# A fused kernel's head: other idle products on TensorE, expert folds moved among them, three small reorderings

## The chip, the cores and the metric

One NeuronCore of one Trainium2 chip runs the whole kernel in one launch. The metric is the device time of that core in microseconds. Three runs of the kernel before gave 267.57, 268.63 and 270.42 us; the median is 268.63 us.

## The reference, cut to what matters

The kernel computes, in float32, a small conditioning network followed by a feed-forward block on 64 samples of 32 rows with 512 features:

```
h    = gelu(gelu(cond @ W0 + b0) @ W1 + b1)              # 64 x 128
att  = softmax(h @ W2 + b2)                               # 64 x 8
agg_w = einsum('bk,koi->boi', att, weight)                # a 32x32 matrix per sample
agg_b = att @ bias_k                                      # 64 x 32
mix  = einsum('boi,bih->boh', agg_w, x) + agg_b[:, :, None]   # 64 x 32 x 512
shared = relu(mix @ up_w)**2 @ down_w                     # 512 -> 1024 -> 512
routed = ((mix @ fc1_w) @ expert_w * top2_sum(mix @ gate_w)) @ fc2_w
out  = x + layernorm(shared + routed) * gamma + beta
```

## The kernel before, in words

The 2048 rows (64 x 32) are 16 tiles of 128 rows, four tiles to a block, so four blocks of 512 rows. The features lie in four chunks of 128 partitions. The instruction order of each engine is written out by hand and the engines meet at semaphores; each engine runs its own list in order.

**Precision.** A float32 value is split into two fp32r parts, `x_hi` (a cast) and `x_lo` (the difference), and `three_products` (L773 to L776) issues hi*hi, hi*lo and lo*hi, each 128x128 weights by up to 512 columns. Small products (the conditioning network, the mix, the expert fold) run on plain float32 operands; such a product is two records in the trace (x2), since TensorE takes it in two parts.

**The head** is all that comes before the first up product. TensorE: H1 (L725), gelu on ScalarE (L402), H2 (L728), gelu (L404), LOGIT (L732, and its bias b2 as a product with a row of ones, L733), softmax on VectorE and ScalarE (L512, L410, L514, L516), transpose of the attention (L740), split of it on VectorE (L520, L522), the eight aggregation products AGG (L746), which give every sample's 32x32 matrix, the rows of the bias (L752), and AGG_B (L755), the bias broadcast over the first block's columns, whose operand VectorE prepares (L527, L533, L535). ScalarE (L433) and VectorE (L569) copy the aggregated matrices into the block-diagonal tile `mix`. Then `mix_chunk` (L758) multiplies x by it, four tiles for each of four feature chunks, on float32. VectorE adds the bias (`mix_bias`, L556), ScalarE casts (`mix_high`, L425), VectorE subtracts (`mix_low`, L561), and the first block's up products (`up_first_block`, L783) begin. The up weights are split on the way: ScalarE casts a quarter (256 columns, `up_hi`, L416), VectorE subtracts it (`up_lo`, L542), in pieces of 128 columns of which each up group m needs its own.

**Idle products.** `stay_warm(n)` (L711) issues n products on TensorE whose result nobody reads. In the kernel before their weights are `gate_hl[:, 0, :]`, 96 columns of zeros on 128 partitions, and they move 192 columns of the same tile. They stand in the head wherever TensorE waits for another engine or a load.

**The expert fold.** `fold_expert(lc, half, m)` (L716) multiplies expert_w and fc2_w once (eight products of 128x128 weights by 256 columns, float32), into PSUM banks 6 and 7. Its result is first needed in the down stage of block 0. Before, two of the eight stand in the head, one behind the third mix chunk, and five in front of the second half of block 0's up products.

From there on TensorE runs up, latent, gate, mix of the next block, and down, four times; the last normalisation and store close the kernel.

Of the kernel before, what the change touches and what calls it, by code (L numbers as in the profile page):

```python
# [5 lines left out]
def adaln_ffn_kernel(  # L6
# [42 lines left out]
    P = 128  # L49
# [30 lines left out]
    with ctx:  # L80
# [85 lines left out]
        ones = sq_lo[0:2 * K, 1, 0:P]  # L166
        half = sb("half", [P, 1])
        warm = sb("warm", [P, 1])

        ps = ctx.enter_context(nc.psum_tensor("ps", [P, 8, TOK], fp32))  # L170
        H1 = ps[:, 4, 64:64 + NB]
        H2 = ps[:, 4, 128:128 + NB]
        LOGIT = ps[0:NB, 4, 192:192 + K]
        ATT_T = ps[0:SR, 4, 256:256 + NB]
        IDLE = ps[0:GC, 0, 0:2 * GC]
        AGG_B = ps[:, 1, :]
        AGGB_ROWS = ps[0:NB, 3, 0:C]

# [216 lines left out]
        @block.scalar  # L395
        def _(act):

            act.wait_ge(dve_const, 1)
            nc.scalar.activation(warm[:, :], warm[:, :], ACT.Gelu).then_inc(warmed, 1)
            act.wait_ge(mlp_loaded, 16)  # L400
            act.wait_ge(h1_done, 1)
            nc.scalar.activation(hid1[:, :], H1, ACT.Gelu, bias=b0_sb).then_inc(gelu_done, 1)  # L402
            act.wait_ge(h2_done, 1)
            nc.scalar.activation(hid2[:, :], H2, ACT.Gelu, bias=b1_sb).then_inc(gelu_done, 1)  # L404

            act.wait_ge(warmed, 1)
            nc.scalar.activation(warm[:, :], warm[:, :], ACT.Exp).then_inc(warmed, 1)
            act.wait_ge(logit_done, 1)
            act.wait_ge(max_done, 1)
            nc.scalar.activation(att_exp[:, :], LOGIT, ACT.Exp, bias=neg_max[:, :],  # L410
                                 accum_out=exp_sum[:, :]).then_inc(exp_done, 1)

            def split_up(i):
                cols = slice(i * UPC, (i + 1) * UPC)
                act.wait_ge(up_loaded[i], 16)
                nc.scalar.copy(up_hi[:, :, cols], up_raw[:, :, cols]).then_inc(up_hi_ready, 1)  # L416

            def q_high(lc):
                act.wait_ge(q_done, lc + 1)
                nc.scalar.copy(q_hi[:, lc, :], Q[lc]).then_inc(q_hi_ready, 1)  # L420

            def mix_high(b, chunks=range(HC)):
                for c in chunks:
                    act.wait_ge(h_ready, HC * b + c + 1)
                    nc.scalar.copy(h_hi[:, c, :], h_full[:, c % 2, :]).then_inc(h_hi_ready, 1)  # L425

            act.wait_ge(const_ready, 2)
            act.wait_ge(agg_done, 1)  # L430
            for q in (0, 1):
                for g in range(G):
                    nc.scalar.copy(mix_part(g, q), agg_src(q, g, TB)).then_inc(mix0_act, 1)  # L433
            split_up(0)
            act.wait_ge(aggb_done, 1)
            nc.scalar.copy(agg_b[:, 0:TOK], AGG_B).then_inc(aggb_copied, 1)
            act.wait_ge(rows_done, 1)
            nc.scalar.copy(aggb_rows[:, :], AGGB_ROWS).then_inc(rows_copied, 1)
            split_up(1)
            mix_high(0, [0])  # L440
            mix_high(0, [1, 2, 3])
            split_up(2)
            split_up(3)
            for q in (0, 1):
                for g in range(G):
                    nc.scalar.copy(agg_part(g, q), agg_src(q, g, NT)).then_inc(agg_act, 1)
            act.wait_ge(latents_loaded, 16)
            nc.scalar.copy(fc1_hi[:, :, :], fc1_raw).then_inc(fc1_hi_ready, 1)
            act.wait_ge(dve_const, 2)
            nc.scalar.copy(gate_hl[:, :, 0:NE], gate_raw).then_inc(gate_hi_ready, 1)  # L450

            def relu_square(b, m):
                act.wait_ge(up_done, IC * b + m + 1)

                wait_past(act, sq_lo_ready, IC * b + max(m - 1, 0))
                nc.scalar.activation(relu_sq[:, m % 2, :], ps[:, UP_BANK[m], :], ACT.Relu).then_inc(relu_done, 1)  # L456
                act.wait_ge(relu_done, IC * b + m + 1)
                nc.scalar.activation(relu_sq[:, m % 2, :], relu_sq[:, m % 2, :], ACT.Square).then_inc(square_done, 1)  # L458

            def latent_gate(b):  # L460
                for lc in range(LC):
                    act.wait_ge(lat_done, LC * b + lc + 1)
                    nc.scalar.copy(lat_hi[:, lc, :], ps[:, LAT_BANK[lc], :]).then_inc(lat_hi_ready, 1)
                act.wait_ge(gate_done, b + 1)
                nc.scalar.copy(gate_sb, ps[0:2 * NE, GATE_BANK, :]).then_inc(gate_copied, 1)

            def scale_routed(b):
                act.wait_ge(top2_done, b + 1)
                for t in range(TB):
                    act.wait_ge(routed_done, TB * b + t + 1)  # L470

                    wait_past(act, final_done, TB * b + max(t - 1, 0))
                    nc.scalar.mul(y_buf[:, t % 2, :], routed(t), top2[:, t:t + 1]).then_inc(scaled_done, 1)  # L473

            def down_high(i):
                ks = slice(i * DNC, (i + 1) * DNC)
                act.wait_ge(down_loaded[i], 16)
                nc.scalar.copy(down_hi[:, ks, :], down_raw[:, ks, :]).then_inc(down_hi_ready, 1)

            for m in range(IC):  # L480
                relu_square(0, m)
                if m in (0, 1):
                    q_high(m)
                if m in (2, 3, 4, 5):
                    down_high(m - 2)
            latent_gate(0)
            mix_high(1)
            scale_routed(0)
            with act.Fori(1, NBLK - 1) as b:
                for m in range(IC):  # L490
                    relu_square(b, m)
                latent_gate(b)
                mix_high(b + 1)
                scale_routed(b)
            for m in range(IC):
                relu_square(NBLK - 1, m)
            latent_gate(NBLK - 1)
            scale_routed(NBLK - 1)

        @block.vector  # L500
        def _(dve):
            nc.vector.memset(warm[:, :], 0.0).then_inc(dve_const, 1)
            nc.vector.memset(gate_hl[:, :, :].bitcast(mybir.dt.uint32), 0).then_inc(dve_const, 1)
            nc.vector.memset(ones[:, :].bitcast(mybir.dt.uint32), ONE_BITS).then_inc(dve_const, 1)
# [62 lines left out]
            for q in (2, 3):  # L567
                for g in range(G):
                    nc.vector.tensor_copy(mix_part(g, q), agg_src(q, g, TB)).then_inc(mix0_dve, 1)  # L569
            split_up(0, 2)  # L570
            dve.wait_ge(aggb_copied, 1)
            mix_bias(0, 0)
            split_up(2)
            mix_low(0, 0)
            mix_bias(0, 1)
            split_up(3)
            mix_low(0, 1)
# [132 lines left out]
        def _(pe):  # L710
            def stay_warm(n):  # L711

                for i in range(n):
                    nc.tensor.matmul(IDLE, gate_hl[:, 0, :], gate_hl[:, 1:3, :], start=True, stop=True)  # L714

            def fold_expert(lc, half, m):  # L716

# [1 line left out]
                return nc.tensor.matmul(Q[lc][:, cols], expert_T[:, m, lc * P:(lc + 1) * P],  # L719
                                        fc2_raw[:, m, cols], start=(m == 0), stop=(m == LC - 1))  # L720

            pe.wait_ge(dve_const, 3)
            stay_warm(11)
            pe.wait_ge(mlp_loaded, 16)
            nc.tensor.matmul(H1, w0_sb, cond_T, start=True, stop=True).then_inc(h1_done, 1)  # L725
            stay_warm(5)
            pe.wait_ge(gelu_done, 1)
            nc.tensor.matmul(H2, w1_sb, hid1[:, :], start=True, stop=True).then_inc(h2_done, 1)  # L728
            stay_warm(4)
            pe.wait_ge(kernels_loaded, 16)  # L730
            pe.wait_ge(gelu_done, 2)
            nc.tensor.matmul(LOGIT, hid2[:, :], w2_sb, start=True, stop=False)  # L732
            nc.tensor.matmul(LOGIT, ones[0:1, 0:NB].bitcast(fp32), b2_sb, start=False, stop=True).then_inc(logit_done, 1)  # L733
            stay_warm(1)
            pe.wait_ge(experts_loaded, 16)
            fold_expert(0, 0, 0)
            stay_warm(1)
            pe.wait_ge(const_ready, 1)
            pe.wait_ge(att_done, 1)
            nc.tensor.transpose(ATT_T, att[:, :], ident[0:NB, 0:NB]).then_inc(attT_done, 1)  # L740
            fold_expert(0, 0, 1)

            pe.wait_ge(weight_lo_ready, 1)
            pe.wait_ge(att_lo_ready, 1)
            for c in range(C // G):
# [4 lines left out]

            pe.wait_ge(attT_copied, 1)
            nc.tensor.matmul(AGGB_ROWS, att_T[0:K, :], bias_raw[0:K, :], start=True, stop=True).then_inc(rows_done, 1)  # L752
            stay_warm(1)
            pe.wait_ge(attb_lo_ready, 1)
            nc.tensor.matmul(AGG_B, ones[:, :], bias_parts, start=True, stop=True).then_inc(aggb_done, 1)  # L755
            stay_warm(3)

            def mix_chunk(b, c, bank):  # L758
                for t in range(TB):
# [8 lines left out]
            mix_chunk(0, 1, MIX0_BANK[1])  # L768
            pe.wait_ge(h_ready, 1)
            mix_chunk(0, 2, MIX0_BANK[2])  # L770
            fold_expert(0, 1, 0)

            def three_products(dst, a_hi, a_lo, b_hi, b_lo, first, last):  # L773
                nc.tensor.matmul(dst, a_hi, b_hi, start=first, stop=False)  # L774
# [8 lines left out]
            def up_first_block():  # L783

                for c in range(HC):
# [10 lines left out]
                    if c == 0:  # L796
                        pe.wait_ge(h_ready, 2)
                        mix_chunk(0, 3, MIX0_BANK[3])
                fold_expert(0, 1, 1).then_inc(q_done, 1)
                pe.wait_ge(h_ready, 3)  # L800
                for half in (0, 1):
                    for m in range(LC):
# [166 lines left out]
```

## Time and profile before

| | us |
|---|---|
| median of three runs | 268.63 |
| lowest, highest | 267.57, 270.42 |
| span of the profiled execution | 266.2 |
| TensorE busy in it | 259.0 (97%) |
| VectorE, ScalarE, GpSimd busy | 154.9, 85.2, 44.6 |
| first TensorE instruction | 1.49 |
| first mix product, first up product | 13.60, 18.24 |

The profile page has no time of its own for the profiled execution beside its span, from the first to the last instruction, 266.2 us. The three timed runs are 1.37, 2.43 and 4.22 us above it; what lies around the span and what differs from run to run can't be told apart there.

A row of the timeline is: start, duration in us, engine, line, operation, written tile and read tiles, shape. xN means N instructions in a row on that engine with nothing of another kind between them, and the duration is then that of the whole group, from the first start to the last end. Matmuls are pipelined, so the end of one lies after the start of the next; the distance of starts is what a product costs. PEld is the load of a product's weights, a separate instruction that TensorE runs beside the matmuls.

### The profile page before, as it was taken

To read this page: it belongs to the slowest core of one execution; us is meant where nothing else is said; L and a number is where in the kernel's file an instruction comes from. 1 tells how busy PE (TensorE), PEld (TensorE's weight loads), DVE (VectorE), ACT (ScalarE), POOL (GpSimd) and SP (SyncE) were. 2 spreads that over 40 slices of the span, in tenths; PEclk is the share of its full clock that TensorE was granted. 3 is DMA by queue.
4 is the path that set the end of the run, shared out by engine and by line. 5 is a ranking of instruction groups with operands and counts; after the bars stand their busy time and mean duration, and the time that the engine had idled before them with its cause. 6 is when DMAs were issued, how large, how long until landed. Compare 5 with 4: busy or idle time off the path is not lost.

```text
span 266.2 us, 3377 instructions
## 1 busy us (share of the span) xinstructions
PE 259.0 (97%) x1222; PEld 215.7 (81%) x1222; DVE 154.9 (58%) x268; ACT 85.2 (32%) x146; POOL 44.6 (17%) x42
## 2 busy tenths in 40 slices
PE   7999999999999999999999999999999999999991
PEld 7698888788888888888888888888888888778891
DVE  3686899974444954384544963384444963314454
ACT  4356994441111354241110354231110355211110
POOL 1000409101111800001111810001111700001111
PEclk9999999999999999999999999999999999999997
DMA  6973710400111240000111140000111100001111
GB/s 211 342 224 147 264 52 10 151 0 0 42 39 39 49 151 0 0 0 4 39 39 39 42 155 0 0 0 0 39 39 39 42 0 0 0 2 39 39 39 39
DMA packets 9132, 15.71 MB, mean 59 GB/s; under 512 B 634, under 2 KB 3578, under 8 KB 9122
## 3 DMA queue, kind: packets, MB, share of 16 engines
q1 hardware_dynamic: 9122, 15.57, 17.4%
q8 instruction: 7, 0.11, 0.2%
q14 instruction: 3, 0.02, 0.0%
HBM read 11.37 MB, written 4.20 MB: 58 GB/s over the span
## 4 chain that ended last, share of the span: by engine, by line
PE 95%; issue 2%; DVE 1%; POOLq 0%; POOL 0%; DVEq 0%
PE ps L774 26%; PE ps L776 26%; PE ps L775 26%; PE ps L760 6%; PE ps L714 2%; PE ps L719 2%; PE ps L838 1%; PE ps L840 1%; PE ps L746 1%; PE ps L850 1%; POOLq L80 0%; POOL rstd L378 0%; PE ps L755 0%; DVE stats L617 0%; DVE y_buf L615 0%
## 5 line engine op out<-in xcount | busy, mean ns | idle before, releaser
L774 PE MATMUL ps<-down_hi,sq_hi 128*128 128x512 f32 (+1 forms) x136 | 51.3, 377 | 0.0
L775 PE MATMUL ps<-down_lo,sq_hi 128*128 128x512 f32 (+1 forms) x136 | 51.2, 377 | 0.0
L776 PE MATMUL ps<-down_hi,sq_lo 128*128 128x512 f32 (+1 forms) x136 | 51.2, 377 | 0.0
L774 PE MATMUL ps<-h_hi,up_hi 128*128 128x512 f32 x128 | 50.3, 393 | 0.0
L776 PE MATMUL ps<-h_hi,up_lo 128*128 128x512 f32 x128 | 49.8, 389 | 0.0
L775 PE MATMUL ps<-h_lo,up_hi 128*128 128x512 f32 x128 | 49.8, 389 | 0.0
L378 POOL TENSOR_TENSOR rstd<-mv,half 128x1 f32<-128x1 f32 x16 | 15.7, 982 | 177.4 <-DVE mv L622 171.9
L456 ACT ACTIVATE relu_sq<-ps 128x512 f32<-128x512 f32 x32 | 19.1, 597 | 58.1 <-PE ps L776 44.2
L615 DVE TENSOR_TENSOR y_buf<-ps,y_buf 128x512 f32<-128x512 f32 x15 | 10.4, 691 | 45.9 <-PE ps L776 45.9
L589 DVE CAST sq_hi<-relu_sq 128x512 fp32r<-128x512 f32 x32 | 23.6, 737 | 20.9 <-ACT relu_sq L458 20.2
L473 ACT ACTIVATE y_buf<-ps,top 128x512 f32<-128x512 f32 x16 | 11.0, 689 | 69.2 <-PE ps L776 67.2
L591 DVE TENSOR_TENSOR sq_lo<-relu_sq,sq_hi 128x512 fp32r<-128x512 f32 x32 | 31.0, 967 | 1.1
L775 PEld LDWEIGHTS ps<-down_lo,sq_hi 128*128 128x128 f32 x136 | 25.6, 188 | 4.7
L774 PEld LDWEIGHTS ps<-down_hi,sq_hi 128*128 128x128 f32 x136 | 25.6, 188 | 4.7
L776 PEld LDWEIGHTS ps<-down_hi,sq_lo 128*128 128x128 f32 x136 | 25.6, 188 | 4.6
L776 PEld LDWEIGHTS ps<-h_hi,up_lo 128*128 128x128 f32 x128 | 24.0, 188 | 5.0
L775 PEld LDWEIGHTS ps<-h_lo,up_hi 128*128 128x128 f32 x128 | 24.0, 188 | 5.0
L774 PEld LDWEIGHTS ps<-h_hi,up_hi 128*128 128x128 f32 x128 | 24.0, 188 | 5.0
L371 POOL TENSOR_TENSOR late<-x_cur,affine_sb 128x2048 f32<-128x2048 f32 x4 | 18.9, 4714 | 10.5 <-DVE down_lo L664 7.6
L458 ACT ACTIVATE relu_sq<-relu_sq 128x512 f32<-128x512 f32 x32 | 20.2, 632 | 1.0
L760 PE MATMUL ps<-mix,x_cur 128*128 128x128 f32 x128 | 18.0, 297 | 0.0
L760 PEld LDWEIGHTS ps<-mix,x_cur 128*128 128x128 f32 x128 | 16.8, 209 | 1.2 <-DMA x_cur<-in_x_dram 0.3
(105 smaller groups left out, 302.4 us busy)
## 6 DMA issues: line engine op xcount, KB each, us to landing
x_cur<-in_x_dram SPq DMA_DIRECT2D x4, 1024.0 KB, 5.5
out_dram<-late SPq DMA_DIRECT2D x15, 256.0 KB, 2.0
late<-in_up_w_dram SPq DMA_DIRECT2D x4, 512.0 KB, 10.0
late<-in_down_w_dram SPq DMA_DIRECT2D x4, 512.0 KB, 5.3
experts_sb<-in_experts_dram SPq DMA_DIRECT2D x1, 768.0 KB, 5.1
agg_b<-aggb_dram SPq DMA_DIRECT2D x1, 768.0 KB, 8.1
latents_sb<-in_latents_dram SPq DMA_DIRECT2D x1, 528.0 KB, 3.9
affine_sb<-in_affine_dram SPq DMA_DIRECT2D x1, 512.0 KB, 5.4
```

Source lines behind the costliest of these rows:

```text
L371: nc.gpsimd.tensor_tensor(x_beta, x_cur[:, :, :], beta_b.unsqueeze(1).to_broadcast([P, TB, HID]), ALU.add).then_inc(xbeta_ready, 1)
L378: nc.gpsimd.tensor_tensor(rstd[:, :], mv[:, 1:2], half[:, :], ALU.pow).then_inc(rstd_done, 1)
L456: nc.scalar.activation(relu_sq[:, m % 2, :], ps[:, UP_BANK[m], :], ACT.Relu).then_inc(relu_done, 1)
L458: nc.scalar.activation(relu_sq[:, m % 2, :], relu_sq[:, m % 2, :], ACT.Square).then_inc(square_done, 1)
L473: nc.scalar.mul(y_buf[:, t % 2, :], routed(t), top2[:, t:t + 1]).then_inc(scaled_done, 1)
L589: nc.vector.tensor_copy(sq_hi[:, m, :], relu_sq[:, m % 2, :]).then_inc(sq_hi_ready, 1)
L591: nc.vector.tensor_tensor(sq_lo[:, m, :], relu_sq[:, m % 2, :], sq_hi[:, m, :].bitcast(fp32), ALU.subtract).then_inc(sq_lo_ready, 1)
L615: nc.vector.tensor_tensor(y, shared(t), y, ALU.add).then_inc(y_done, 1)
L760: last = nc.tensor.matmul(ps[:, bank, t * P:(t + 1) * P], x_cur[:, t, c * P:(c + 1) * P], mix[:, t, :], start=True, stop=True)
L774: nc.tensor.matmul(dst, a_hi, b_hi, start=first, stop=False)
L775: nc.tensor.matmul(dst, a_hi, b_lo, start=False, stop=False)
L776: return nc.tensor.matmul(dst, a_lo, b_hi, start=False, stop=last)
```

## The change

The idle products get a tile of their own, `idle`, 128x128 fp32r filled with ones by VectorE as its first instruction, and each is now 128 columns of weights by 128 moved columns. Their numbers go from 11, 5, 4, 1, 1, 1, 3 (26 in all) to 20, 8, 8, 10, 6, 24 (76 in all). TensorE begins when the `idle` tile is set; before, it waited for three memsets. The bias product of the logits is issued ahead of the product with hid2, before the wait for the second gelu, and LOGIT goes from PSUM bank 4 to bank 2. Four expert folds stand in the head instead of two, and none between the third mix chunk and the first up product. On ScalarE the copy of the bias tile (`agg_b`) comes ahead of the first quarter's cast, and the first `h_hi` cast ahead of the second quarter's. On VectorE the first up split is one piece of 128 columns instead of two, and the bias add comes ahead of the second.

```diff
+        idle = sb("idle", [P, P], f32r)
-        LOGIT = ps[0:NB, 4, 192:192 + K]
+        LOGIT = ps[0:NB, 2, 0:K]
-        IDLE = ps[0:GC, 0, 0:2 * GC]
+        IDLE = ps[:, 0, 0:P]
...
-            split_up(0)
             act.wait_ge(aggb_done, 1)
             nc.scalar.copy(agg_b[:, 0:TOK], AGG_B).then_inc(aggb_copied, 1)
+            split_up(0)
             act.wait_ge(rows_done, 1)
             nc.scalar.copy(aggb_rows[:, :], AGGB_ROWS).then_inc(rows_copied, 1)
+            mix_high(0, [0])
             split_up(1)
-            mix_high(0, [0])
...
+            nc.vector.memset(idle[:, :].bitcast(mybir.dt.uint32), ONE_BITS).then_inc(dve_const, 1)
             nc.vector.memset(warm[:, :], 0.0).then_inc(dve_const, 1)
...
-            split_up(0, 2)
+            split_up(0)
             dve.wait_ge(aggb_copied, 1)
             mix_bias(0, 0)
+            split_up(1)
+            mix_low(0, 0)
             split_up(2)
-            mix_low(0, 0)
...
-                    nc.tensor.matmul(IDLE, gate_hl[:, 0, :], gate_hl[:, 1:3, :], start=True, stop=True)
+                    nc.tensor.matmul(IDLE, idle[:, :], idle[:, :], start=True, stop=True)
...
-            pe.wait_ge(dve_const, 3)
-            stay_warm(11)
+            pe.wait_ge(dve_const, 1)
+            stay_warm(20)
             pe.wait_ge(mlp_loaded, 16)
             nc.tensor.matmul(H1, w0_sb, cond_T, start=True, stop=True).then_inc(h1_done, 1)
-            stay_warm(5)
+            stay_warm(8)
             pe.wait_ge(gelu_done, 1)
             nc.tensor.matmul(H2, w1_sb, hid1[:, :], start=True, stop=True).then_inc(h2_done, 1)
-            stay_warm(4)
             pe.wait_ge(kernels_loaded, 16)
+            pe.wait_ge(dve_const, 4)
+            nc.tensor.matmul(LOGIT, ones[0:1, 0:NB].bitcast(fp32), b2_sb, start=True, stop=False)
+            stay_warm(8)
             pe.wait_ge(gelu_done, 2)
-            nc.tensor.matmul(LOGIT, hid2[:, :], w2_sb, start=True, stop=False)
-            nc.tensor.matmul(LOGIT, ones[0:1, 0:NB].bitcast(fp32), b2_sb, start=False, stop=True).then_inc(logit_done, 1)
-            stay_warm(1)
+            nc.tensor.matmul(LOGIT, hid2[:, :], w2_sb, start=False, stop=True).then_inc(logit_done, 1)
+            stay_warm(10)
             pe.wait_ge(experts_loaded, 16)
             fold_expert(0, 0, 0)
-            stay_warm(1)
+            fold_expert(0, 0, 1)
+            stay_warm(6)
             pe.wait_ge(const_ready, 1)
             pe.wait_ge(att_done, 1)
             nc.tensor.transpose(ATT_T, att[:, :], ident[0:NB, 0:NB]).then_inc(attT_done, 1)
-            fold_expert(0, 0, 1)
-
+            fold_expert(0, 1, 0)
...
-            stay_warm(1)
+            fold_expert(0, 1, 1).then_inc(q_done, 1)
             pe.wait_ge(attb_lo_ready, 1)
             nc.tensor.matmul(AGG_B, ones[:, :], bias_parts, start=True, stop=True).then_inc(aggb_done, 1)
-            stay_warm(3)
+            stay_warm(24)
...
             mix_chunk(0, 2, MIX0_BANK[2])
-            fold_expert(0, 1, 0)
...
-                fold_expert(0, 1, 1).then_inc(q_done, 1)
```

TensorE's list from the second layer of the conditioning network to the aggregation, before (L714 is an idle product, L728 H2, L732 and L733 LOGIT and its bias, L719 an expert fold, L740 the transpose, L746 AGG):

```order
L728 MATMUL ps<-hid,mlp_sb 128x64
L714 MATMUL ps<-gate_hl 96x192 x4
L732 MATMUL ps<-mlp_sb,hid 64x8
L733 MATMUL ps<-kernels_sb,sq_lo 64x8
L714 MATMUL ps<-gate_hl 96x192
L719 MATMUL ps<-experts_sb 128x256
L714 MATMUL ps<-gate_hl 96x192
L740 MATMUL ps<-ident,relu_sq 40x64
L719 MATMUL ps<-experts_sb 128x256
L746 MATMUL ps<-sq_hi 128x64 x8
```

The same place in the changed kernel (L717 idle product, L731 H2, L734 bias, L737 LOGIT, L722 fold, L745 transpose, L750 AGG):

```order
L731 MATMUL ps<-hid,mlp_sb 128x64
L734 MATMUL ps<-kernels_sb,sq_lo 64x8
L717 MATMUL ps<-idle 128x128 x8
L737 MATMUL ps<-mlp_sb,hid 64x8
L717 MATMUL ps<-idle 128x128 x10
L722 MATMUL ps<-experts_sb 128x256 x2
L717 MATMUL ps<-idle 128x128 x6
L745 MATMUL ps<-ident,relu_sq 40x64
L722 MATMUL ps<-experts_sb 128x256
L750 MATMUL ps<-sq_hi 128x64 x8
```

Between LOGIT and the transpose there were two idle products and a fold; now there are sixteen and two folds.

VectorE's list from the copies of the aggregated matrices on, before (L569 copies, L542 up split, L556 bias add, L561 `h_lo`):

```order
L569 COPY mix<-ps 32x8x4 x8
L542 TENSOR_TENSOR up_lo<-late,up_hi 128x4x256
L556 TENSOR_TENSOR h_full<-ps,agg_b 128x512
L542 TENSOR_TENSOR up_lo<-late,up_hi 128x4x128
L561 TENSOR_TENSOR h_lo<-h_full,h_hi 128x512
```

and in the changed kernel (L571, L544, L558, L563 in the same roles):

```order
L571 COPY mix<-ps 32x8x4 x8
L544 TENSOR_TENSOR up_lo<-late,up_hi 128x4x128
L558 TENSOR_TENSOR h_full<-ps,agg_b 128x512
L544 TENSOR_TENSOR up_lo<-late,up_hi 128x4x128
L563 TENSOR_TENSOR h_lo<-h_full,h_hi 128x512
```

The piece of the split that stands ahead of the bias add is half as wide.

## Rows read from the trace of the kernel before

**Rows 1.** The page: span, and the chain that ended last, by engine.

```profile
span 266.2 us, 3377 instructions
...
PE 95%; issue 2%; DVE 1%; POOLq 0%; POOL 0%; DVEq 0%
```

**Rows 2.** Timeline of TensorE in the head: start us, duration us, what.

```profile
1.49 2.08 PE L714 MATMUL ps<-gate_hl 128*96 128x192 f32 x11 [1.49 <-DVE sq_lo L504]
3.36 0.57 PE L725 MATMUL ps<-mlp_sb 128*128 128x64 f32 x2
...
4.59 0.58 PE L728 MATMUL ps<-hid,mlp_sb 128*128 128x64 f32 x2
...
5.79 0.38 PE L732 MATMUL ps<-mlp_sb,hid 128*64 128x8 f32 x2
...
8.11 0.29 PE L740 MATMUL ps<-ident,relu_sq 64*40 64x64 f32 x1
8.34 1.22 PE L719 MATMUL ps<-experts_sb 128*128 128x256 f32 x2
9.49 1.91 PE L746 MATMUL ps<-sq_hi 40*128 40x64 f32 x8
...
13.60 4.56 PE L760 MATMUL ps<-mix,x_cur 128*128 128x128 f32 x24
...
18.24 0.58 PE L774 MATMUL ps<-h_hi,up_hi 128*128 128x512 f32 x1
```

**Rows 3.** Stretches: us, busy time of each engine, granted clock, DMA.

```profile
13.60:17.05 3.45, 3.45 (x16) 3.45 (x17) 2.51 (x3) 2.94 (x5) 0.00 (x0) 1.00 0.51 152
17.05:20.00 2.95, 2.95 (x19) 2.64 (x19) 2.78 (x5) 0.67 (x2) 0.00 (x0) 1.00 1.04 292
```

**Rows 4.** One line's instructions: ns min/median/max; L760 up to 16.9, then from 50 on.

```profile
L760 PE MATMUL ps<-mix,x_cur x15: 421/421/552, 13.6 to 16.7; 128*128 128x128 f32 x15
...
L760 PE MATMUL ps<-mix,x_cur x32: 275/275/377, 50.7 to 55.1; 128*128 128x128 f32 x32
```

**Rows 5.** One line's instructions: AGG's products and weight loads, the idle products' weight loads.

```profile
L746 PEld LDWEIGHTS ps<-sq_hi x8: 285/330/334, 9.5 to 10.9; 40*128 40x128 f32 x8
L746 PE MATMUL ps<-sq_hi x8: 397/397/419, 9.5 to 11.0; 40*128 40x64 f32 x8
...
L714 PEld LDWEIGHTS ps<-gate_hl x26: 234/277/280, 1.5 to 13.1; 128*96 128x96 f32 x26
```

**Rows 6.** Chain of waits in order of time: start us, us, what.

```profile
30.40 2.16 PE ps L719 x10
...
172.04 2.68 PE ps L760 x24
```

**Rows 7.** Timeline of ScalarE in the head.

```profile
5.20 0.31 ACT L404 ACTIVATE hid<-ps,mlp_sb 128x64 f32<-128x64 f32 x1 [0.85 <-PE ps L728]
...
6.93 0.25 ACT L410 ACTIVATE att_exp<-ps,neg_max 64x8 f32<-64x8 f32 x1
...
13.32 1.04 ACT L416 CAST up_hi<-late 128x1024 fp32r<-128x1024 f32 x1
14.39 0.59 ACT L436 COPY agg_b<-ps 128x512 f32<-128x512 f32 x1
```

**Rows 8.** Timeline of VectorE in the head.

```profile
0.93 0.38 DVE L503 MEMSET gate_hl<- 128x384 uint32 x1
...
7.50 0.25 DVE L516 TENSOR_SCALAR relu_sq<-att_exp,exp_inv 64x40 f32<-64x40 f32 x1
...
10.23 0.68 DVE L535 TENSOR_TENSOR sq_lo<-y_buf,sq_lo 8x512 fp32r<-8x512 f32 x1
11.51 1.94 DVE L569 COPY mix<-ps 32x32 f32<-32x32 f32 x8 [0.60 <-PE ps L746]
14.47 1.23 DVE L542 TENSOR_TENSOR up_lo<-late,up_hi 128x1024 fp32r<-128x1024 f32 x1 [1.02 <-ACT up_hi L416]
15.75 0.69 DVE L556 TENSOR_TENSOR h_full<-ps,agg_b 128x512 f32<-128x512 f32 x1
```

More of the change, by code:

```diff
@@ L396, in _ @@
         def _(act):
-            act.wait_ge(dve_const, 1)
+            act.wait_ge(dve_const, 2)
             nc.scalar.activation(warm[:, :], warm[:, :], ACT.Gelu).then_inc(warmed, 1)
@@ L448, in _ @@
             nc.scalar.copy(fc1_hi[:, :, :], fc1_raw).then_inc(fc1_hi_ready, 1)
-            act.wait_ge(dve_const, 2)
+            act.wait_ge(dve_const, 3)
             nc.scalar.copy(gate_hl[:, :, 0:NE], gate_raw).then_inc(gate_hi_ready, 1)
```

## The prediction

> **What bounds the kernel now.** I read the page first: of the 266.2 us span 95% of the chain that ended last is TensorE [rows 1]. Behind the head its products follow each other without a gap, so only two kinds of edit can matter: when the first up product starts, and how much TensorE work stands behind it. Then the timeline of TensorE in the head: H1 at 3.36, H2 at 4.59, LOGIT at 5.79, transpose at 8.11, AGG at 9.49, mix from 13.60, first up product at 18.24 [rows 2]. Between these stand the idle products, so a "busy" TensorE there says nothing; what matters is the next real product's operand and whether an idle product is in its way.
>
> Next the clock. The mix product lasts 421 ns until 16.7 and 275 ns later on [rows 4]. Its 24 records in the head take 4.56 us [rows 2], 0.21 each in the first stretch (3.45 us, 16 of them [rows 3]); in the steady state 24 take 2.68 us, 0.11 each [rows 6]. That is the lower level (1.2 GHz) up to 17.05 us and the upper (2.4 GHz) from there. The granted-clock column reads 1.00 in both stretches [rows 3]; I go by the durations. So the whole head runs at the lower level although idle products fill it, and the rise comes 3.45 us after the mix products start to run back to back.
>
> **What a new idle product costs.** The old one moves 192 columns and costs (2.08 - 0.36)/10 = 0.17 us, first gap included [rows 2] (0.36 is its own duration there, the group's end behind its last start). A new one moves 128, which by columns alone would be 0.11. But AGG moves only 64 columns, with 128 columns of weights, and costs (1.91 - 0.40)/7 = 0.216 us [rows 2, 5], more than the old idle product with three times its columns. So the weights set that pace: 128 columns of them, 0.21 at the lower clock. The loads' own durations agree, 330 ns for 128 columns against 277 for 96 [rows 5]: 53 ns for 32 columns, 0.21 for 128. The mix record holds 128 weight columns too and costs 0.21 low and 0.11 high. I price the new product at 0.21 low and 0.11 high; the lower bound is 0.11 and 0.055 (moved columns alone). The Trainium skill (TensorE: Matmul & The Clock Gate, LDWEIGHTS) gives a weight load as its columns divided by 1.2, 107 ns for 128 columns, half of what AGG shows; by that the sum would be that of rival F below. No row here shows a load of 128 columns at that pace.
>
> **When the clock rises.** The trace has no dense stretch of such products, so this is bounded. Earliest: 3.45 us after the first one, as with the mix [rows 3], so 1.1 + 3.45 = 4.5 us. Never in the head: the other bound. The old head stayed at the low level with holes (waits for weights after a semaphore, 96 columns, small products of 40, 16 or 8 rows); the new products are full tiles with the mix products' pace, which is the nearest row, and that one was followed by a rise. Against: they move half as long as the mix records do (128 column steps in a float32r product; the mix takes two steps a column: 0.21 for 128). I take a rise between 4.5 and 7.9 (once to twice the 3.45), middle 6.2.
>
> **The sum**, by this.
> (a) TensorE starts at about 1.1 instead of 1.49, as a 128-column memset takes its place for those with 384 (0.38 [rows 8]). 20 products x 0.21 = 4.2, so H1 starts at 5.4; its operands are there at 3.36 at the latest [rows 2]. **+2.0**.
> (b) H1 to H2 was 1.23 (4.59 - 3.36), the gelu's latency. Now 0.4 for H1 and the first gap, and 8 products, part of them at the low clock: 1.4. **+0.15**.
> (c) H2 to transpose was 8.11 - 4.59 = 3.52. Of it, exp starts 1.73 behind the gelu's start (6.93 - 5.20 [rows 7]; ScalarE changes its table between) and the softmax ends 0.82 behind exp (7.75 [rows 8]). Now TensorE is what is late: 1.2 to LOGIT, then 10 x 0.11, two folds of 0.43 ([rows 6]: five in 2.16), 6 x 0.11, gaps of 0.3: 4.1. **+0.6**. The bias moved ahead of LOGIT saves nothing, since exp is held by the table and not by the logits.
> (d) Transpose to AGG was 1.37, because the fold between (1.15 from 8.34 to AGG) outlasts VectorE's split. At the high clock the fold is 0.43 and the split decides: 0.8. **-0.57**.
> (e) AGG to mix was 4.11. Now AGG 0.95 (8 x 0.11), rows and the fourth fold 0.7; AGG_B waits for its operand, which VectorE ends 2.8 behind the transpose (10.91 - 8.11 [rows 8]), 2.0 behind AGG; AGG_B 0.3; then 24 x 0.11 = 2.65: 5.0. The copies into `mix`, 1.94 [rows 8], end 3.1 behind AGG, so the idle products and not the copies hold the mix. **+0.9**. Mix at 16.7.
> (f) Mix to first up product was 4.64. Now chunk 0 lands 1.1 behind the start, the bias add takes 0.69 [rows 8], cast and `h_lo` on tiles of the same size about as long each, with hops: 3.2. **-1.4**; the fold that stood at its end is in this. The smaller first split does little by itself: ScalarE's cast starts 0.59 later behind the bias copy [rows 7], VectorE's piece is 0.6 shorter (half of 1.23 [rows 8]), and at 16.7 the split is long done; the add waits for the mix.
> (g) One fold fewer ahead of the second half of up: **-0.43** [rows 6].
> Sum +1.25: span 267.4 against 266.2. Behind the head nothing moves: `up_lo` pieces are ready within 0.1 us of their use, the loads are issued by semaphores that shift with the head and have microseconds of slack, GpSimd is not in it.
>
> Times: the median is 2.43 above the span, the lowest run 1.37. In the profiled execution the rise came as early as it can after 13.60; in other executions it may come later, so I expect part of the 2.43 to be that, and add 1.7: **269.1 us**. Of its own this case reaches from 268.0 to 270.5 (rise at 4.5 or 7.9 makes -0.8 or +0.85, offsets 1.37 to 2.43).
>
> **Rivals.**
> F, the products cost only their moved columns (0.11 low, 0.055 high) and the clock rises early. H1, H2, LOGIT and transpose stay where they were (20 x 0.11 = 2.1, mlp just loaded), (d) stays at -0.57, 24 fillers take 1.3 and the mix starts at 12.7 behind its copies, the up products at 16.4: -1.85, with (g) -2.3, 263.9 span, time 265.3 to 266.3. For it: the old product's 0.17 for 192 columns [rows 2] fits a price by moved columns. Against: AGG's 0.216. Chance 0.10.
> M, the rise comes late in the head, between 8 and 14 us, when folds and fillers run one behind the other. Each microsecond of delay costs about half: +2.0 to +3.4 on the forecast, minus what overlaps: 271 to 272.6. Chance 0.15.
> C, slower: the new products do not raise the clock, and every one costs 0.21. (a) +2.0; (b) 0.4 + 8 x 0.21 = 2.15, +0.9; (c) bias, 24 fillers (5.1), two folds of about 1.0, small products: 8.2, +4.7; (d) -0.2; (e) AGG 1.85, rows 0.4, fold 1.0, AGG_B 0.6, 24 fillers 5.1: 9.0, +4.9; (f) and (g) -0.4 each. Sum +11.5, mix at 26.0, span 277.7, time 279.1 to 281. For it: the old idle products did not raise it either, and the rise came only with products that move without a pause. It decides from the point where the clock is still low at LOGIT (10.1 us instead of 8.1): each filler behind it then costs 0.1 more. Chance 0.27.
> The rest, 0.03, lies between these.
>
> **The numbers.** Forecast 0.45. A measurement here tells about 1% from no change: below 265.9 is faster, above 271.3 slower. Faster: most of F, 0.09. Same: the forecast, a piece of F and of M: 0.48. Slower: C, most of M, and the rest: 0.43. The range leaves out F but for its top, and the end of C: 266.5 to 280.5; the likeliest case alone is 268.0 to 270.5.
>
> **What would show it.** The distance of the idle products' starts before the rise: 0.21 (mine), 0.11 (F). H1 at 5.4. The mix product's duration in the head: 275 ns everywhere in mine, 421 in C. Transpose near 11.0, AGG to mix near 5.0 with `mix` copies done 1.9 before. First up product near 20. Folds in front of the second half of up: x8 instead of x10. I am wrong if H1 starts at 3.4, or if the mix starts behind 20 us.

## The result, and the profile after

The changed kernel is slower: 280.56 us median (279.32 to 281.85, four runs) against 268.1 us for the kernel before in the same session, ratio 1.0438 with a 95% interval of 1.0362 to 1.0514. The profiled run took 279.39 us with a span of 277.1 us, 10.9 above the span before. That is rival C (279.1 to 281) and not the forecast of 269.1. Every ratio here and below leaves out executions more than 1.5% above the fastest of their kernel (2, 5, 5 and 1 of them in experiments 4, 6, 7 and 9), so it is not the quotient of the medians, which are over all executions.

The timeline of TensorE in the head of the changed kernel (L717 idle products, L728 H1, L731 H2, L737 LOGIT, L722 expert folds, L745 transpose, L750 AGG, L759 AGG_B, L764 mix, L777 first up product), to be laid beside [rows 2]:

```profile
1.06 4.53 PE L717 MATMUL ps<-idle 128*128 128x128 f32 x20 [1.06 <-DVE warm L504]
5.39 0.63 PE L728 MATMUL ps<-mlp_sb 128*128 128x64 f32 x2
...
7.53 0.63 PE L731 MATMUL ps<-hid,mlp_sb 128*128 128x64 f32 x2
...
10.29 0.38 PE L737 MATMUL ps<-mlp_sb,hid 128*64 128x8 f32 x2
10.60 2.40 PE L717 MATMUL ps<-idle 128*128 128x128 f32 x10
12.80 2.02 PE L722 MATMUL ps<-experts_sb 128*128 128x256 f32 x4
14.25 1.35 PE L717 MATMUL ps<-idle 128*128 128x128 f32 x6
15.54 0.23 PE L745 MATMUL ps<-ident,relu_sq 64*40 64x64 f32 x1
...
16.41 1.05 PE L750 MATMUL ps<-sq_hi 40*128 40x64 f32 x8
...
18.33 0.69 PE L759 MATMUL ps<-sq_lo 16*128 16x512 f32 x1
18.95 5.38 PE L717 MATMUL ps<-idle 128*128 128x128 f32 x24
24.13 5.08 PE L764 MATMUL ps<-mix,x_cur 128*128 128x128 f32 x24
28.96 0.47 PE L777 MATMUL ps<-h_hi,up_hi 128*128 128x512 f32 x1
```

Every real product is late because idle products stand in front of it: H1 by 2.03 us, H2 by 2.94, LOGIT by 4.5, the transpose by 7.4, the first up product by 10.7. Twenty idle products take (4.53 - 0.42)/19 = 0.216 us each, first gap included (415 ns is the median duration of one). VectorE had the softmax ready at 11.79, 3.75 us before the transpose, and its copies into `mix` done at 20.24, 3.9 us before the mix:

```profile
11.54 0.25 DVE L518 TENSOR_SCALAR relu_sq<-att_exp,exp_inv 64x40 f32<-64x40 f32 x1
...
18.30 1.94 DVE L571 COPY mix<-ps 32x32 f32<-32x32 f32 x8
```

The stretches show the clock (us, busy time of PE, PEld, DVE, ACT, POOL, granted clock, DMA share, GB/s):

```profile
3.00:12.00 9.00, 9.00 (x44) 8.72 (x43) 2.46 (x5) 2.47 (x6) 0.00 (x0) 1.00 1.03 343
...
15.10:18.40 3.30, 3.27 (x21) 2.28 (x20) 2.43 (x7) 0.77 (x4) 0.00 (x0) 1.00 0.01 3
18.50:24.00 5.50, 5.50 (x25) 5.07 (x25) 2.22 (x9) 2.39 (x7) 0.00 (x0) 0.50 0.22 57
24.00:28.60 4.60, 4.60 (x23) 4.60 (x23) 2.01 (x4) 1.56 (x2) 0.00 (x0) 0.50 1.01 333
28.80:35.00 6.20, 6.20 (x35) 5.29 (x34) 4.73 (x8) 2.38 (x4) 0.00 (x0) 1.00 0.00 1
```

From 18.5 to 28.6 the granted clock is 0.50, the lower level, while TensorE is busy in every slice. Between 15.1 and 18.4 it is 1.00 and means it: the idle products from there on last 273 ns instead of 415, and AGG takes 1.05 us for its eight instead of 1.91 [rows 2]. Before 15 the column also reads 1.00, but the products keep the pace and durations of the lower level; as in the kernel before, that part of the column is no evidence. So the upper level came once in the head, right behind the two expert folds (12.80 to 14.8), and went while small products and waits filled TensorE. The rise that lasts came at 28.7, 4.6 us into the mix. Two of the four runs took 281.7 and 281.9 us, 2.4 more. Their mean granted clock is 0.994 and 0.996, against 0.977 and 0.976 in the two of 279.4 and 279.3; the 10.2 us at the lower level that follow the rise behind the folds in the profiled run are not in their record, so that rise is most likely missing there. There is no profile of them.

### The profile page after: what moved, and what is told of

Its sections match the earlier page's. It is cut to its first block, busy times and chain, and to the rows that moved or that the text cites. A ratio compares the mean times of both kernels' runs of the same rounds, so it can differ in the third digit from the quotient of the medians.

```text
span 277.1 us, 3478 instructions
## 1 busy us (share of the span) xinstructions
PE 269.7 (97%) x1272; PEld 227.0 (82%) x1272; DVE 155.2 (56%) x270; ACT 85.1 (31%) x146; POOL 44.7 (16%) x42
## 4 chain that ended last, share of the span: by engine, by line
PE 82%; DVE 5%; ACT 4%; issue 3%; POOL 2%; DMA 2%; POOLq 0%; DVEq 0%; SPq 0%
PE ps L777 22%; PE ps L779 22%; PE ps L778 22%; PE ps L717 6%; PE ps L764 5%; DMA x_cur<-in_x_dram 2%; POOL late L372 2%; ACT agg L447 1%; PE ps L722 1%; ACT up_hi L417 1%; PE ps L840 1%; DVE sq_lo L594 1%; PE ps L842 1%; DVE h_full L558 1%; ACT h_hi L426 1%
## 5 line engine op out<-in xcount | busy, mean ns | idle before, releaser
L777 PE MATMUL ps<-down_hi,sq_hi 128*128 128x512 f32 (+1 forms) x136 | 51.3, 377 | 0.0
L777 PE MATMUL ps<-h_hi,up_hi 128*128 128x512 f32 x128 | 50.2, 392 | 0.0
L777 PEld LDWEIGHTS ps<-down_hi,sq_hi 128*128 128x128 f32 x136 | 25.6, 188 | 4.7
L777 PEld LDWEIGHTS ps<-h_hi,up_hi 128*128 128x128 f32 x128 | 24.0, 188 | 4.9
L764 PE MATMUL ps<-mix,x_cur 128*128 128x128 f32 x128 | 18.5, 303 | 0.7 <-DVE lat_lo L600 0.4
L764 PEld LDWEIGHTS ps<-mix,x_cur 128*128 128x128 f32 x128 | 17.4, 215 | 1.7 <-DMA x_cur<-in_x_dram 0.8
## 6 DMA issues: line engine op xcount, KB each, us to landing
late<-in_up_w_dram SPq DMA_DIRECT2D x4, 512.0 KB, 10.1
```

The lines of the kernel that those rows point to most:

```text
L764: last = nc.tensor.matmul(ps[:, bank, t * P:(t + 1) * P], x_cur[:, t, c * P:(c + 1) * P], mix[:, t, :], start=True, stop=True)
```

## The experiments

All were run beside the kernel before; the ratio is to its runs in the same session, and "rises at" is where the durations halve in the profiled run (where the clock's record begins there, the column agrees). Medians of the kernel before were 269.38, 268.72 and 268.9 us in the three sessions. Except where said, the edit is made on the changed kernel, and its other parts stay.

**1. Twice the moved columns, same weights.** Here and in 2 and 4 the one line that matters:

```diff
-  nc.tensor.matmul(IDLE, idle[:, :], idle[:, :], start=True, stop=True)
+  nc.tensor.matmul(IDLE, idle[:, 0:128], idle[:, 0:256], start=True, stop=True)   # 1
+  nc.tensor.matmul(IDLE, idle[:, 0:96], idle[:, 0:192], start=True, stop=True)    # 2
+  nc.tensor.matmul(IDLE, idle[:, 0:64], idle[:, 0:128], start=True, stop=True)    # 4
```

> The changed kernel, with 256 moved columns in each idle product instead of 128; weights and counts as in the change. Theory A (the load of 128 weight columns sets the pace, 0.213 us at the low clock, and the clock rises only for products that move all the time, which 128 moved columns do half the time): the idle products keep their distance of 0.213 us, so the schedule up to the rise is the same to a hundredth (H1 at 5.4), but the clock rises between 4.5 and 8 us; mix at 16 to 17.5, time 268 to 270. Theory B (idle products of whatever density never raise it): same trace as the change, 279 to 282. Theory C (moved columns set the pace): the distance becomes 0.43 and the time goes over 290.

Measured: 272.8 us (272.23 to 272.99), ratio 1.0132 [1.0074, 1.0189], 7.8 us below the change. Its timeline and stretches:

```profile
1.20 4.04 PE L717 MATMUL ps<-idle 128*128 128x256 f32 x20 [1.20 <-DVE warm L504]
...
18.73 3.06 PE L764 MATMUL ps<-mix,x_cur 128*128 128x128 f32 x24
```

```profile
4.40:14.60 10.20, 10.17 (x69) 8.52 (x69) 5.47 (x15) 3.86 (x13) 0.00 (x0) 1.00 1.04 349
14.70:18.00 3.30, 3.30 (x17) 3.30 (x17) 1.63 (x6) 1.79 (x4) 0.00 (x0) 0.50 0.09 25
```

It rises at 4.37, inside the first twenty, and from there a product with 256 moved columns costs about 0.11 us. Before the rise it keeps 0.213: twice the moved columns for the same price. Theories B and C fall. The clock fell at 14.61 behind AGG, the bias rows and AGG_B, which move 32 or 64 columns or use 16 to 40 rows, and came back at 18.02; with it the 24 products in front of the mix ran at the low level, the mix started 1.2 us above the expected 16 to 17.5, and in block 1 TensorE waited 1.0 us for the next x. The time is 2.8 us over the top of the range. All four runs lie within 0.8 us and 6 us or more below those of the change, so a rise in the head is no exception of the profiled one. In two of them a mean granted clock of 0.998 or more leaves no room for the fall.

**2. The old shape in the new numbers.**

> The changed kernel with the shape of the old idle product: 96 weight columns, 192 moved (but ones, from the new tile); counts of the change. Distance 0.16 us at the low clock in every theory. Theory A, with columns of the array not counting: the clock rises between 4.5 and 8 us, mix at 14 to 15.4, time 266.5 to 268.5. Theory A': three quarters of the array's columns are not enough (what the words 'full 128x128 tile' say): no rise before the folds, mix near 21, first up product near 26, time 275 to 278. Theory B: the same as A'.

Measured: 269.82 us (268.95 to 271.88, ten runs), ratio 1.0048 [1.0007, 1.0089]. It rises at 5.24 and stays:

```profile
1.13 3.52 PE L717 MATMUL ps<-idle 128*96 128x192 f32 x20 [1.13 <-DVE warm L504]
4.44 0.58 PE L728 MATMUL ps<-mlp_sb 128*128 128x64 f32 x2
...
9.96 0.23 PE L745 MATMUL ps<-ident,relu_sq 64*40 64x64 f32 x1
...
15.42 3.08 PE L764 MATMUL ps<-mix,x_cur 128*128 128x128 f32 x24
18.77 0.47 PE L777 MATMUL ps<-h_hi,up_hi 128*128 128x512 f32 x1 [0.27 <-issue]
```

So a rise came here with 96 of the 128 weight columns, and Theory A' falls. With the same shape in fewer products, 11, 5 and 4 in front of the logits, none came before 17.05 in the kernel before and 21.26 in experiment 5. The head is at the high clock from 5.24, and still the first up product starts at 18.77, 0.53 later than before [rows 2]: H1 has lost 1.1 us to twenty products, the transpose 1.85. The time is 1.3 us above Theory A's range: the mix is at its upper end, and TensorE waited 0.8 us for the next x ahead of block 1's mix.

**3. The old numbers in the new shape** (20, 8, 8, 10, 6, 24 become 11, 5, 4, 1, 1, 3).

> The changed kernel with the counts of idle products of the kernel before (11, 5, 4, 1, 1, 3), in the new shape. It tells the number of products from all the rest. Theory A: low clock until the mix has run for 3.4 us or more, H1 at 3.5, mix near 15, first up product near 19.5; time 268.5 to 271. If the moved folds and the reorderings and not the counts cost the 11 us, it stays above 278.

Measured: 270.99 us (269.65 to 271.87), ratio 1.0064 [1.0035, 1.0093]; H1 at 3.47, mix at 16.70, first up product at 20.99. The 11 us are gone. The mix is 1.7 us later than expected; 0.8 of it is the first fold's wait for the load of its operands, and behind it the folds run at the lower level:

```profile
8.45 2.08 PE L722 MATMUL ps<-experts_sb 128*128 128x256 f32 x4 [0.78 <-DMA experts_sb<-in_experts_dram]
```

**4. Half the weights.**

> The changed kernel with 64 weight columns and 128 moved columns in an idle product. Theory A's price: the load of 64 columns takes 0.107 us at the low clock, so the distance halves to 0.107, H1 at 3.4. Price by moved columns at two steps each: it stays 0.213, H1 at 5.4. For the clock: if moving all the time is enough with half of the array's columns, the rise comes between 4.5 and 8 us, mix near 12.7, time 265.5 to 267; if it wants all columns, no rise before the folds, mix near 17.9, time 271 to 274.

Measured: 270.71 us (267.51 to 273.8), ratio 1.0 [0.9953, 1.0046].

```profile
1.06 2.40 PE L717 MATMUL ps<-idle 128*64 128x128 f32 x20 [1.06 <-DVE warm L504]
3.26 0.63 PE L728 MATMUL ps<-mlp_sb 128*128 128x64 f32 x2
...
13.55 2.82 PE L717 MATMUL ps<-idle 128*64 128x128 f32 x24
16.17 3.42 PE L764 MATMUL ps<-mix,x_cur 128*128 128x128 f32 x24
```

```profile
13.40:16.70 3.30, 3.30 (x28) 3.15 (x27) 2.10 (x8) 2.26 (x7) 0.00 (x0) 0.50 0.41 131
```

(2.40 - 0.3)/19 = 0.11 us for a product that moves the same 128 columns: the 128 weight columns were the price. In the profiled run it rises only at 9.97, behind the two folds, falls at 13.38 and rises again at 16.80. This product moves all the time but holds 64 weight columns. It doesn't decide whether that keeps the clock down: the same products were followed by no rise in the 6.8 us before the folds, yet they fill 2.6 of the 3.4 us ahead of the rise at 16.80. And two of the ten runs took 267.51 us, 3.2 less than the profiled one, at a mean granted clock of 0.999 instead of 0.989; there is no profile of them.

**5. All but the idle products** (old shape and numbers; folds, bias and orders of the change).

> All of the change but its idle products: these have the old shape (96 weight columns, 192 moved) and the old counts (11, 5, 4, 1, 1, 3); moved folds, bias first, the orders on ScalarE and VectorE stay. Theory A (idle products alone cost the time, the rest is worth little because the block 1 load of x follows ScalarE's and VectorE's chain and not TensorE's): equal to the kernel before within 1%, 267.5 to 270.5; TensorE waits 0.5 to 1.0 us for x_cur ahead of block 1's mix. If the fold taken from ahead of the second half of up counted in full, and nothing else did, 0.4 us below before and no such wait.

Measured: 271.09 us (268.97 to 271.94), ratio 1.0035 [0.9993, 1.0078]: no difference that can be told, and if any a loss; the median is 0.6 us above the expected range. The profiled run shows where one can come from, the waits of TensorE:

```profile
PE ps L722 <- DMA experts_sb<-in_experts_dram: 1.7, 1, 1.7
...
PE ps L764 <- DMA x_cur<-in_x_dram: 0.4, 1, 0.4
PE ps L764 <- DVE lat_lo L600: 0.3, 1, 0.3
```

The experts landed at 8.7 here and by 6.8 before; behind that wait two low-clock folds (2.08 us) and not one stand ahead of the transpose, which comes at 10.89.

**6 and 7. Dense products in fitted numbers** (128 weights, 256 moved, 10, 4, 3, 2, 1, 10), and 7 with the first two quarters of the down weights split ahead of the fold's result:

```diff
-                if m in (0, 1):
-                    q_high(m)
-                if m in (2, 3, 4, 5):
-                    down_high(m - 2)
+                if m in (2, 3):
+                    q_high(m - 2)
+                if m in (0, 1, 4, 5):
+                    down_high(m - 2 if m > 1 else m)
...
```

(the same on VectorE with `q_low` and `down_low`).

> The dense idle product (128 weight columns, 256 moved) with counts cut to the latencies: 10, 4, 3, 2, 1, 10. Theory A: H1 at 3.4, the clock rises between 4.5 and 8 us and AGG and mix run at the high clock, transpose at 7.9 to 8.4, mix near 13 (VectorE's copies into mix, behind its bias operands, then set it), first up product near 16.5 to 17; TensorE then waits for x_cur, and the time is 265.5 to 267.5. Theory B (cut counts leave holes, the clock doesn't hold): the rise comes at 17 or later, 268 to 270.

> As e6_fit256, and ScalarE and VectorE split the first two quarters of the down weights ahead of the fold's result (m = 0, 1 instead of 2, 3), so that GpSimd may start x + beta, and SyncE the next load of x_cur, two steps earlier. Theory A: x + beta starts 3 us or more earlier against the first up product, the wait for x_cur goes from 0.5-1.0 us to nothing, time 0.4 to 1.0 us below e6_fit256. Rival: something else is due at the same moment (lat_lo, copies into mix) and the time doesn't change.

Measured: 6 took 272.39 us (268.39 to 273.93), ratio 1.0015 [0.9956, 1.0073]; 7 took 270.75 (267.89 to 273.32), ratio 1.0036 [0.9975, 1.0097]. Over all ten runs the median of 6 is 1.4% above that of the kernel before, and of 7 0.8%; 6 is above the ranges of both its theories. Both scatter over 5.5 us, and the two profiles show a likely reason: 6 rises only at 20.0, its mix at 17.17; 7, with the same head, rises at 5.21, falls at 12.03, 0.9 us before its mix, and rises again at 15.45. The same list of TensorE was followed by an early rise in one execution and not in the other. In 7 the next x is issued at 41.43 instead of 48.99, relative to the first up product 24.2 instead of 27.6 us, and TensorE waits for other things:

```profile
PE ps L777 <- ACT relu_sq L457: 0.6, 1, 0.6
PE ps L764 <- DVE lat_lo L600: 0.4, 1, 0.4
```

From the first up product to block 1's mix 7 takes 32.77 us, 6 takes 32.86. The rival holds: the load's wait (0.8 us in 6) went, one for relu took its place. The times of 6 and 7 can't tell it, since the moment of the rise moves them more.

**8. Zeros instead of ones** (as 2).

> As e2_old_form (old shape, counts of the change), the idle tile filled with zeros instead of ones. If the values don't matter for the clock: rise between 4.3 and 8 us as in e2_old_form, 269 to 272. If zeros don't count as activity: no rise before the folds, 275 to 278.

Measured: 270.89 us (269.61 to 271.85), ratio 1.0063 [1.0017, 1.0109]; it rises at 5.80. Zeros were followed by an early rise as ones were (one profile each).

**9. No fold ahead of the transpose** (dense products 10, 4, 3, 7, 3; one fold behind the bias rows, three behind AGG_B in place of idle products).

> Dense idle product (128 weight columns, 256 moved), counts 10, 4, 3, 7, 3, and no expert fold ahead of the transpose: one behind the bias rows, three behind AGG_B, where they take the place of idle products. Theory A (e5 and e6 lost time because two folds at the low clock, and the landing of the experts, stand ahead of the transpose): transpose at 7.8 to 8.3 wherever the experts land, mix at 12.8 to 13.3 at the high clock, 14 to 15 at the low one; span 265 to 266.5 where the clock rises early, time 0.3 to 1% below the kernel before. Rival (the copies into mix and the split of the first up quarter set the start of the up products anyway): within 0.3% of before.

Measured: 268.29 us (267.18 to 271.2, twelve runs), ratio 1.0004 [0.9967, 1.0041]. Seven runs lie between 267.2 and 268.4, five between 270.9 and 271.2. In the profiled run (span 265.9) the transpose is at 7.67, and the mix at 13.29 begins in a stretch that has fallen back:

```profile
10.88 2.62 PE L722 MATMUL ps<-experts_sb 128*128 128x256 f32 x6
13.29 3.72 PE L761 MATMUL ps<-mix,x_cur 128*128 128x128 f32 x24
```

It is the best of the versions here, and the same as the kernel before: the head of Theory A came, but its gain did not. TensorE waited 0.8 us for the next x ahead of block 1's mix.

**10. The kernel before with dense idle products only** (10, 4, 3, 1, 1, 1, 6).

> The kernel before, with nothing of the change but denser idle products (128 weight columns, 256 moved, counts 10, 4, 3, 1, 1, 1, 6) and the start at 1.1. Theory A: the clock rises early in some executions only, since the holes behind LOGIT stay; a gain of 0 to 0.6%. Rival: the early rise doesn't depend on density, or doesn't come at all; same as before within 0.2%.

Measured: 269.92 us (267.82 to 271.54), ratio 1.0021 [0.9995, 1.0048]; the profiled run rises at 17.84, and its first fold waited 1.2 us for the load of its operands. No gain: the rival.

**11. The kernel before with the change's idle products only.**

> The kernel before with the change's idle products alone: 128 weight columns, 128 moved, counts 20, 8, 8, 10, 6, 1, 24 in the places of the kernel before; folds, bias product and the orders of ScalarE and VectorE stay as before. Theory A: all the loss is here: H1 at 5.4, mix at 23 to 26, time 279 to 282. If the moved folds made part of the loss: 1 us or more below the change's 280.6.

Measured: 279.65 us (two runs, 279.13 and 280.17), ratio 1.0388 [1.0346, 1.043]. Idle products alone give the whole loss, within the interval:

```profile
1.07 4.53 PE L716 MATMUL ps<-idle 128*128 128x128 f32 x20 [1.07 <-DVE warm L504]
...
14.87 0.29 PE L743 MATMUL ps<-ident,relu_sq 64*40 64x64 f32 x1
...
19.56 5.38 PE L716 MATMUL ps<-idle 128*128 128x128 f32 x24
24.74 5.13 PE L763 MATMUL ps<-mix,x_cur 128*128 128x128 f32 x24
```

Here a fold of 1.16 us and none of the change's second one precedes the transpose, and no early rise came; the rise is at 29.4.

## Why the prediction was right and wrong, point by point

**The price of an idle product was right.** 0.21 us, from AGG's pace and the weight loads [rows 2, 5]; measured 0.213 to 0.216 with 128 or 256 moved columns (change, 1) and 0.11 with 64 weights (4). Rival F is out. The 107 ns for a load of 128 columns, which the prediction took from the Trainium skill (TensorE: Matmul & The Clock Gate, LDWEIGHTS), is not what these 4-byte weights show at the lower level: products with 128 of them start 0.213 us apart, and 0.11 only at the upper one.

**The step that failed is "When the clock rises".** I took a rise between 4.5 and 7.9 us because the new products have the mix's pace and tile. In the profiled run none came before 15.05, and LOGIT (at 10.29, C's 10.1), the 24 idle products behind AGG_B and nearly the whole mix ran at the lower level; the mix started at 24.13, past the 20 us that the prediction had named as its sign of being wrong. The times say the same of the runs without a profile: the four of the change and the two of 11 lie between 279.1 and 281.9, the four of 1, whose profile has the early rise, between 272.2 and 273.0.

The rows on both sides: twenty products of 128 weight by 128 moved columns in 4.5 us, and twenty-four in 5.2 us at a granted clock of 0.50, were not followed by a rise. With 256 moved columns at the same 0.213 us, and nothing else changed, it came at 4.37 (1); with 96 by 192 at 5.24 (2) and 5.80 (8). So the point that I had put against my own reading, that the new products move half as long as the mix records do, is the one that 1 bears out. The full tile, for which I had taken the pace of the mix as the nearest row, was not needed (2). Whether fewer weight columns than 96 are enough stays open (4). A row of products that was followed by a rise once need not be the next time: 6 and 7. And 3.45 us was not the earliest, as I had it: in 1 and 9 the rise came 3.2 us behind the first idle product.

The stated range, 266.5 to 280.5, reaches to the result only because it took in most of rival C. The case that the forecast stands for, 268.0 to 270.5, was missed by 10 us, so that nearness is luck and not foresight; the chances were 0.45 for the case that did not come and 0.27 for the one that did.

**The sum of rival C, by steps.** (a) +2.0, measured +2.03. (b) H1 to H2 2.15, measured 2.14. (c) 8.2, measured 8.01 (7.53 to 15.54). (d) 1.2 in C, measured 0.87, since the clock was up. (e) 9.0, measured 7.7: AGG 1.0, rows, fold and AGG_B in 1.6 at the high clock, 24 products in 5.2. (f) Mix to first up product 4.2 by C, measured 4.83: the 24 mix records took 5.08, all but the last few at the low clock, where before eight ran at the high one. The sum was +11.5, the span moved by +10.9: the 3.4 us at the high clock between 15.05 and 18.46, which rival C did not have, took off more than (f) and (g) added.

**(g) was wrong.** The fold fewer ahead of the second half of up was to save 0.43 and "behind the head nothing moves". From the first up product to block 1's first mix product it took 32.42 us before (50.66 - 18.24) and 32.31 after (61.27 - 28.96), 0.11 less and not 0.43; from there to the end it took 215.5 us before and 215.9 after. TensorE had no wait in either stretch before, and these two after, the first ahead of block 1's mix, the second inside it:

```profile
PE ps L764 <- DMA x_cur<-in_x_dram: 0.3, 1, 0.3
PE ps L764 <- DVE lat_lo L600: 0.4, 1, 0.4
```

So (g) came out as a loss of 0.2. The chain of waits of the changed kernel shows what came in its place:

```profile
49.83 1.15 DVE down_lo L667
...
51.22 4.66 POOL late L372
...
56.08 5.15 DMA x_cur<-in_x_dram
61.23 0.04 issue
61.27 1.17 PE ps L764 x8
62.45 0.04 DVEq L293
62.48 0.29 DVE lat_lo L600
```

The load of the next x waits for GpSimd's x + beta, that for VectorE's split of the down weights, and this chain follows ScalarE's and VectorE's work, not TensorE's. I had called that slack microseconds. In the kernel before the load is issued 5.52 us ahead of block 1's first mix product, and it takes 5.15 in the changed one, so the slack was about 0.4:

```profile
45.14 0.39 SPq L321 DMA_DIRECT2D x_cur<-in_x_dram  x1
```

In 2 the stretch is 32.87, in 3 32.97, in 1 33.14: what TensorE gains in the head beyond that chain it gives back here, in 7 to relu instead.

**(c) and (e), what is late next, were right in kind.** At the high clock (2) the fillers and folds and not the softmax hold the transpose (softmax ready at 8.69, transpose at 9.96). For (e) I had let the copies into `mix` end 3.1 behind AGG; in 2 they end 3.86 behind it (14.70 against 10.84), since VectorE runs them behind the bias operands, so the mix can hardly start earlier than 4 us behind AGG; in 7 it starts 4.02 behind it, the closest of the profiles. That, and not only the idle products, is a reason why a high clock buys so little in this head.

## What to carry to other kernels

An idle product has its price like any other: here 0.213 us at the lower level for 128 weight columns, whether 128 or 256 columns move, and 0.11 for 64. Count it against the latency that it is to fill, at the pace that a row shows for the same number of weight columns. For the clock, look for a row of the same shape that was followed by a rise, moved columns included, and not for one of the same pace: here 128 by 256 had one and 128 by 128 at the same 0.213 us had none. Test that first with the schedule unchanged (experiment 1) before adding more of them, and over several executions, since one profile can show either (6 and 7). And before a product is taken off TensorE's list, look up which load or chain is due right behind it: here a load with 0.4 us of slack took the gain.

## What the runs showed of the hardware that was not expected

- The granted-clock column is empty of evidence before its first record: it reads 1.00 from 0 to 15 us in the changed kernel while idle products run at 0.213 us, and 0.50 only from 18.46, with the same pace.
- The upper level is lost in the middle of a busy head: in 1 at 14.61, in the change at 18.46, in 4 at 13.38, in 7 at 12.03, in 9 at 11.23, each time during AGG_B or within 1.3 us of its start, behind AGG and the bias rows, while TensorE shows as busy (8 to 40 rows; 32 or 64 moved columns, 512 in AGG_B). In 2 and 8 the same products stand in the same order and no fall followed. The level came back 3.4 us later in 1, 4, 7 and 9, and 10.2 us later in the change, where idle products of 128 by 128 followed.
- A product of few moved columns costs by its 4-byte weight columns: 0.11 us for 64 and 0.213 for 128 at the low clock, 0.11 for 128 at the high one.
- The same kernel varies with the moment of the rise: 9 takes 267.2 to 268.4 us in seven runs and 270.9 to 271.2 in five. The profiled one (268.12, rise at 4.41, fall at 11.23) has a mean granted clock of 0.990; so have, within 0.001, the other five between 268.1 and 268.4, while all five from 270.9 on have 0.995. So the slower five have no early rise with such a fall in their record; where theirs came, no profile tells.
